# Maxima reduced with their sign turned, one VectorE copy out of PSUM, and the split into three bfloat16 rows on GpSimd

## The reference, cut to what matters

```python
h = embed(x); h = h + attn_rank10(layernorm(h))          # stage 1
spatial_out  = spatial_experts(layernorm(h), idx_s)       # "S": softmax(q k^T) v, 8 heads
temporal_out = temporal_experts(layernorm(h), idx_t)      # "T": the same, causal
fused = cross_mha(spatial_out, temporal_out)              # "C": the same, q of S, keys of T
x = x + fused                                             # stage 2 up to here
x = x + mlp(layernorm(x))                                 # stage 3
```

## Time and profile before

| what | value |
|---|---|
| runs | 1793.36, 1794.24, 1794.6 us; median 1794.24 |
| the profiled execution | 1795.07 us, of it a span of 1793.2 us from first to last instruction |
| busy, PE | 1589.7 us, 89% of the span |
| busy, PEld | 728.6 us, 41% |
| busy, DVE | 1276.4 us, 71% |
| busy, ACT | 1208.4 us, 67% |
| busy, POOL | 697.1 us, 39% |
| mean granted TensorE clock | 0.926 of full speed |

### The profile page before, as it was taken

One profiled execution on the slowest core, in us unless ns is written; L12 is line 12 of the kernel. 1 busy time (PEld: TensorE's weight loads), 2 busy tenths in 40 slices (PEclk: granted clock), 3 DMA queues, 4 the chain that ended last, 5 costly groups with the idle time before them and its releaser, 6 DMA issues. The chain is left out here.

```text
span 1793.2 us, 36960 instructions
## 1 busy us (share of the span) xinstructions
PE 1589.7 (89%) x9638; PEld 728.6 (41%) x9638; DVE 1276.4 (71%) x3087; ACT 1208.4 (67%) x2377; POOL 697.1 (39%) x673
## 2 busy tenths in 40 slices
PE   3669947889999999999999999999999999855998
PEld 1217933333344343434434344334434343211665
DVE  6986856378787877878787787878787787452442
ACT  3325741757878778787878878787888878714333
POOL 7823441234344344344344334434434433221442
PEclk9559965889999999999999999999999999957999
DMA  2211125354564555465456456456455545030122
GB/s 51 73 44 37 47 54 71 42 80 62 63 77 65 66 71 77 53 78 73 56 71 78 65 60 85 59 64 77 64 67 71 76 50 72 2 36 26 58 60 58
DMA packets 132338, 109.25 MB, mean 61 GB/s; under 512 B 21824, under 2 KB 125248, under 8 KB 132288
## 3 DMA queue, kind: packets, MB, share of 16 engines
q1 hardware_dynamic: 130240, 104.44, 41.5%
q0 software_dynamic: 2048, 4.20, 0.9%
HBM read 19.26 MB, written 8.39 MB: 15 GB/s over the span
## 5 line engine op out<-in xcount | busy, mean ns | idle before, releaser
L1034 ACT ACTIVATE probs<-psum 128x512 f32<-128x512 f32 (+3 forms) x1536 | 737.8, 551 | 268.3 <-PE psum L1143 158.4
L915 DVE TENSOR_REDUCE mx_S<-psum 128x1 f32<-128x512 f32 x512 | 323.5, 684 | 74.6 <-PE psum L1128 72.7
L915 DVE TENSOR_REDUCE mx_C<-psum 128x1 f32<-128x512 f32 x512 | 317.5, 683 | 53.0 <-PE psum L1128 51.6
L915 DVE TENSOR_REDUCE mx_T<-psum 128x1 f32<-128x128 f32 (+3 forms) x512 | 240.6, 488 | 119.7 <-PE psum L1131 107.6
L847 POOL TENSOR_TENSOR rem_q<-f_q,parts_q 128x512 f32<-128x512 f32 x48 | 55.4, 1155 | 495.8 <-ACT parts_q L1020 479.2
L1128 PE MATMUL psum<-ks_S,qs_S 96*128 96x512 bf16 x512 | 201.7, 400 | 18.0 <-DMA ks_S<-parts_k 13.7
L1128 PE MATMUL psum<-ks_C,qs_C 96*128 96x512 bf16 x512 | 203.0, 398 | 12.4 <-DMA ks_C<-parts_k 7.3
L1143 PE MATMUL psum<-qs_C,ks_C 99*128 99x512 bf16 x512 | 193.6, 389 | 18.1 <-ACT probs L1034 11.5
L1143 PE MATMUL psum<-qs_S,ks_S 99*128 99x512 bf16 x512 | 195.9, 384 | 1.6 <-ACT probs L1034 0.9
L1128 PE MATMUL psum<-ks_T,qs_T 96*128 96x128 bf16 (+3 forms) x512 | 157.6, 310 | 7.4 <-DMA ks_T<-parts_k 6.0
L1143 PE MATMUL psum<-qs_T,ks_T 99*128 99x256 bf16 (+3 forms) x512 | 153.6, 302 | 7.6 <-ACT probs L1034 6.4
(11 more groups left out here) (188 smaller groups left out, 2702.3 us busy)
## 6 DMA issues: line engine op xcount, KB each, us to landing
qs_S<-parts_q SPq DMA_DIRECT2D x96, 128.0 KB, 4.2
ks_S<-parts_k SPq DMA_DIRECT2D x96, 128.0 KB, 6.8
qs_T<-parts_q SPq DMA_DIRECT2D x96, 128.0 KB, 4.4
ks_T<-parts_k SPq DMA_DIRECT2D x96, 128.0 KB, 6.8
qs_C<-parts_q SPq DMA_DIRECT2D x96, 128.0 KB, 4.4
ks_C<-parts_k SPq DMA_DIRECT2D x96, 128.0 KB, 6.8
w_in_S<-in_s_in SPq DMA_DIRECT2D x16, 257.0 KB, 2.7
w_in_T<-in_t_in SPq DMA_DIRECT2D x16, 257.0 KB, 2.7
```

What stands on the lines that cost most here:

```text
L915: nc.vector.tensor_reduce(mx[kind][:, n:n + 1], psum[:, ring_place(kind, b, n, RL), 0:last_key], AX_X, ALU.max)\
L1034: nc.scalar.activation(probs[:, n // 4 % 2, n % 4, t0:T], psum[:, LOGITS + ring_place(kind, b, n, RC), t0:T], ACT.Exp, scale=SCALE).then_i ...
```

## The change

`reduce` now writes each maximum negated (`negate=True`). `negate` on DVE is left with one copy of the 32x128 block from PSUM into `ng`, which frees the desk; before it, it waits until POOL has done with the `ng` of the unit before. The wait for the landed rows and the four steps of the split are now in `split_maxima` on POOL, at the head of each slot, ahead of `split`. `neg_step` counts four per unit where it counted five. In the diff the first part is SP's, the next two are POOL's and the last two DVE's.

```diff
                 def slot_program(i, slot):
...
-                        sp.wait_ge(neg_step, 5 * (unit_no(kb, bb) + 1))
+                        sp.wait_ge(neg_step, 4 * (unit_no(kb, bb) + 1))
...
+                def split_maxima(kind, b):
+                    u = unit_no(kind, b)
+                    pool.wait_ge(desk_free, desk_use("m" + kind, b) + 1)
+                    if before(kind, b):
+                        pk, pb = before(kind, b)
+                        pool.wait_ge(rows_in[pk], 16 * NPART * (pb + 1))
+                    pool.sem_inc(maxima_seen, 1)
+                    nc.gpsimd.tensor_copy(ng_p[:, 0, :], ng[:]).then_inc(neg_step, 1)
+                    pool.wait_ge(neg_step, 4 * u + 1)
+                    nc.gpsimd.tensor_tensor(ng_r[:], ng[:], ng_p[:, 0, :], ALU.subtract).then_inc(neg_step, 1)
+                    pool.wait_ge(neg_step, 4 * u + 2)
+                    pool.sem_inc(maxima_seen, 1)
+                    nc.gpsimd.tensor_copy(ng_p[:, 1, :], ng_r[:]).then_inc(neg_step, 1)
+                    pool.wait_ge(neg_step, 4 * u + 3)
+                    nc.gpsimd.tensor_tensor(ng_p[:, 2, :], ng_r[:], ng_p[:, 1, :], ALU.subtract).then_inc(neg_step, 1)
...
                 def slot_program(i, slot):
+                    if exists(bb):
+                        split_maxima(kb, bb)
                     split(kn, bn)
...
-                    nc.vector.tensor_reduce(mx[kind][:, n:n + 1], psum[:, ring_place(kind, b, n, RL), 0:last_key], AX_X, ALU.max)\
-                        .then_inc(reduced, 1)
+                    nc.vector.tensor_reduce(mx[kind][:, n:n + 1], psum[:, ring_place(kind, b, n, RL), 0:last_key], AX_X, ALU.max,
+                                            negate=True).then_inc(reduced, 1)
 
                 def negate(kind, b):
                     dve.wait_ge(desk_full, desk_use("m" + kind, b) + 1)
-                    nc.vector.tensor_scalar(ng[:], desk[0:TILES, 0:P], -1.0, None, ALU.mult).then_inc(desk_free, 1)
-                    dve.wait_ge(desk_free, desk_use("m" + kind, b) + 1)
                     if before(kind, b):
-                        pk, pb = before(kind, b)
-                        dve.wait_ge(rows_in[pk], 16 * NPART * (pb + 1))
-                    nc.vector.tensor_copy(ng_p[:, 0, :], ng[:]).then_inc(neg_step, 1)
-                    dve.wait_ge(neg_step, 5 * u + 1)
-                    nc.vector.tensor_tensor(ng_r[:], ng[:], ng_p[:, 0, :], ALU.subtract).then_inc(neg_step, 1)
-                    dve.wait_ge(neg_step, 5 * u + 2)
-                    nc.vector.tensor_copy(ng_p[:, 1, :], ng_r[:]).then_inc(neg_step, 1)
-                    dve.wait_ge(neg_step, 5 * u + 3)
-                    nc.vector.tensor_tensor(ng_p[:, 2, :], ng_r[:], ng_p[:, 1, :], ALU.subtract).then_inc(neg_step, 2)
+                        dve.wait_ge(neg_step, 4 * u)
+                    nc.vector.tensor_copy(ng[:], desk[0:TILES, 0:P]).then_inc(desk_free, 1)
```

More of the change, by code:

```diff
@@ L697, in attend @@
         reduced = sem("reduced2")
-        neg_step = sem("neg_step2")
+        neg_step, maxima_seen = sem("neg_step2"), sem("maxima_seen")
         logits_in = sem("logits_in2")
@@ L852, in split @@
                             .then_inc(lo_done, 1)
+                def split_maxima(kind, b):
[13 more added lines that the diff above has]
+                    nc.gpsimd.tensor_tensor(ng_p[:, 2, :], ng_r[:], ng_p[:, 1, :], ALU.subtract).then_inc(neg_step, 1)
                 def slot_program(i, slot):
-                    (kn, bn), _, _, (ko, bo) = units(i, slot)
+                    (kn, bn), _, (kb, bb), (ko, bo) = units(i, slot)
+                    if exists(bb):
+                        split_maxima(kb, bb)
                     split(kn, bn)
```

## The result

| | before | after |
|---|---|---|
| median of the runs, us | 1794.17 (1793.36 to 1796.43, 12 runs) | 1797.88 (1796.21 to 1800.36, 12 runs) |
| the profiled execution, us | 1795.07, span 1793.2 | 1797.45, span 1795.5 |

The ratio is 1.002, with a 95% interval of 1.0011 to 1.0029: slower by 3.7 us, at the edge of what a measurement of this kernel can tell. Predicted were 0.35 us and no change. The size is inside the range; the point is 3.3 us off.

What follows compares the result with a forecast made beforehand. PE was taken to bound the slots. Later rows at fill and drain, 2.65 us, less 2.3 gained from DVE's relief, gave +0.35 us: predicted median 1794.6 us, own range 1791 to 1798, over cases 1789 to 1802.

Steps and rivals of the forecast that it cites:

- the gain: PE's stop for a DVE reduction in 14 steady C slots: DVE's relief gives back 0.16 us each, 2.3 us.
- My lower bound: Least gain from DVE's relief at PE's stop in C slots: nothing, if another limit stands right behind.
- The negated reduction and the copy: DVE's remaining steps: turning the reduction's sign costs zero, and the copy takes 0.27 us like the multiplication it replaces.
- That rival (1804): DVE's negated reduction costs 0.05 us more a tile, some 10 us together: 1804 us, chance 0.05.
- POOL's prices: POOL's split: 0.32 us a copy, 0.43 a subtraction, 2.05 from copy's end to first row DMA; rows 0.75 later.
- Hidden in the loop: Rows 0.75 us later cost nothing in 44 of 48 slots; the C slot has 0.93 us to spare.
- The ends: Fill and drain, where PE waits for rows: 0.75 us each in S 0, C 14, C 15, 0.4 in T 0; sum 2.65.
- may pay a part: The last T slot, with nothing left to project, may pay part of the 0.75 us row delay; left to the range.
- Faster (0.12): DVE's relief also reaches PE's other stops: 1787 us with C and S slots, 1776 with T too; chance 0.12.
- Slower by late rows: Rows too late in C slots, as at twice POOL's estimated step times or with a shared SBUF port: 1810, 1808 to 1820; chance 0.16.

Runs made afterwards that it cites:

- e3: The changed kernel with VectorE also doing the four split steps, into tiles that nothing reads: 1808.05 us, ratio 1.0019 to the kernel before.
- e1: The kernel before with only the negated reduction and the copy, the split staying on VectorE: 1803.77 us, ratio 1.0004 to the kernel before.
- e6: The changed kernel with one more 32x128 subtraction on POOL ahead of the low part, in the loop only: 1798.75 us, ratio 1.002 to the kernel before.
- e7: The changed kernel with three more 32x128 subtractions on POOL ahead of the low part, in the loop only: 1819.02 us, ratio 1.0136 to the kernel before.

## Why the prediction was right or wrong

**The step that failed is the gain:** "By the last paragraph PE gets back 0.16 us in each of 14 C slots: 14 x 0.16 = 2.3 us". The stop was there and DVE was the one waited for, but the split wasn't its cause. In the kernel after it stays, with DVE idle 1.49 us just before; with the split's load put back (e3) it is 0.22 us; the loop differs by 0.2 us between kernels with and without it. The trace of before held it already, inside the merged row of six reductions in the earlier trace rows. Cut to one reduction each (timeline, DVE, kernel before):

```profile
832.44 0.69 DVE L915 TENSOR_REDUCE mx_S<-psum 128x1 f32<-128x512 f32 x1
...
833.05 0.68 DVE L915 TENSOR_REDUCE mx_S<-psum 128x1 f32<-128x512 f32 x1
...
833.83 0.69 DVE L915 TENSOR_REDUCE mx_S<-psum 128x1 f32<-128x512 f32 x1
```

The third starts 0.10 us after the second has ended, on the tile that PE gave at 833.40. DVE had worked off the split's backlog and waited for PE. This third reduction ends at 834.52, and PE's stop, for a tile three later, ends at 834.58. In the kernel after the same reduction starts 2.95 us behind the start of the copy, here 2.95 behind that of the sign change. In e3 it starts 3.02 behind, since its steps take longer, and the stop is longer by about as much, 0.05. What makes the stop is a burst of PE: around step 5 the second pass of T runs tiles of 128 columns, PE takes a step in about 0.33 us (loads of L1138 at 832.89 and 833.23), and the reductions (four in 2.48 us) take 0.62 each, with three banks between them. What a fourth bank would give back stays open, since that kernel changed too much. My lower bound, "nothing, if another limit stands right behind", was the right one.

**The negated reduction and the copy** cost nothing, as predicted: 683 ns against 684, 0.269 us for the copy against the 0.27 taken, and e1 for the sum. That rival (1804) falls.

**POOL's prices** were right. The cast took 0.28 us (0.32 estimated), the subtraction 0.416 and 0.418 (0.43), copy's end to first row DMA 2.00 us (2.05), so the rows come 0.69 us later where I had 0.75.

**Hidden in the loop:** right. No wait of PE for rows appears there, and e6 shows that half a us more is hidden too. Rows land at 832.35 + 1.22 + 1.9 = 835.47 and the first tile runs at 835.87, 0.40 us to spare. That is the 1.09 us that I read before less the delay of 0.69; the 0.16 by which PE was to come earlier did not have to be taken off.

**The ends** were mis-sized. Of the terms that I named, C 14 and C 15 came as predicted (0.7 us each in the waits), S 0 and T 0 can't be told from the spread of the fill (-0.1 and +0.8 us from S 0 to C 0, where I had 1.15), and the last T slot, which "may pay a part", paid 0.3 us. Not foreseen were the drain, 1.0 us, and the third block, 0.5 us: both kernels do the same work there, so I had given them nothing. From C 13 to the end 1.5 us was forecast and 3.0 measured. The clock rows show where the drain's went. Observed from S 0 on: +2.6 and +3.5 us in the two executions, against a forecast of +0.35 of which 2.65 were the ends. That 2.65 stands so near to the observed is partly luck: the fill showed less than its term and the tail twice its own. Without the gain the prediction would have been 1796.9, and about the unforeseen drain is left to the measured 1797.9. That 1797.9 lies in the range is no proof of the working, since the range is wider than both terms.

**The rivals.** Faster (0.12) falls with the gain. Slower by late rows did not come: the delay was 0.69. But its price was wrong, and e7 shows how: "It decides from 0.93 us of delay for PE and from about 1.5 for the time, since PE has slack before ACT" is false. At a delay of 2.25 us I had C slots losing 0.75 and "S and T slots little", 10.5 us in the loop; e7 had 0.69 + 1.56, the very 2.25, and lost 21.7. PE's 0.52 us before the exponential took up only about half of itself, 0.25 us in e6 and 0.28 in e7, and S and T slots had 1.2 to 1.3 us of slack and no more. Nor do the rival's "1808 to 1820" follow from its own formula, which gives 1806 and 1823 for delays of 2 and 3 us. Its mechanism, DVE and POOL sharing a port, doesn't hold for reductions out of PSUM: they kept 683 ns, and POOL's steps came at the prices estimated without it. Read as the prediction read it, the shared port that it cited from the Trainium skill (Perfetto Trace Analysis, "Optimizing Scalar/DVE Operations") would have given the slower rival; the trace of the kernel after shows no such wait for these two partners.

## What to carry to other kernels

A stop of the bounding engine for another names the partner, not the cause. Look at the very instruction that it waited for: if that one had itself started late for want of the bounding engine's tile, relieving the partner buys nothing. A merged row can hide such a gap, and putting the load back (e3) settles it. Latency that a pipeline hides in its steady slots is paid in its fill and drain, so count it there first, and look for serial issues that can start on parts of the data, as the row DMAs could. Slack is counted up to the first consumer on the bounding engine, and a later wait of that engine took up only a quarter of a microsecond more. A stop there costs more than the idle time shown, as a matmul's overlap with its neighbour is lost too: e7's rows kept PE waiting 1.8 us a round, 0.7 of which was taken up elsewhere, and the round still paid 1.67.

## What the runs showed of the hardware

**POOL's steps slow DVE's on SBUF, but not DVE's reductions out of PSUM.** In e3 both engines do the same four small steps at once. Groups of DVE in e3 (busy us, mean ns of one, idle):

```profile
L956 DVE TENSOR_TENSOR idle_p<-idle_r,idle_p 32x128 bf16<-32x128 f32 x48 | 19.6, 408 | 5.0
L954 DVE CAST idle_p<-idle_r 32x128 bf16<-32x128 f32 x48 | 19.0, 397 | 1.7
L952 DVE TENSOR_TENSOR idle_r<-ng,idle_p 32x128 f32<-32x128 f32 x48 | 14.1, 295 | 1.6
L950 DVE CAST idle_p<-ng 32x128 bf16<-32x128 f32 x48 | 10.3, 215 | 5.9 <-DVE ng L946 2.0
```

The first cast and subtraction took 215 and 295 ns; the second ones, beside POOL's, 397 and 408. In the kernel before they took 214 and 279. The reductions in e3 kept 682 ns, and POOL's own steps 281 and 419 to 420 ns. The page "SBUF — State Buffer" of the Trainium skill, section "SBUF: two separate sides", says that a GpSimd operation and a DVE one shut each other out for a whole instruction, if DVE's is in a two-port mode or has two SBUF inputs and GpSimd's reads SBUF: the one that starts first gets the shared ports. The rows agree as far as DVE is the one shut out: its second subtraction lost 0.13 us and its second cast 0.18. None shows POOL shut out, and none shows in which mode DVE's cast ran.

**POOL's hand-over to itself** cost 0.08 us between a cast and a subtraction and 0.17 between a subtraction and a cast with a semaphore increment between; its start behind DVE's copy 0.25 us (830.35 to 830.60).
